# A four-layer kernel on one Trainium2 core: the start of the program in another order

## The reference

```python
x = x + mixer(layernorm(x), W_in, conv_w, ..., W_out)      # Mamba-2: 32 heads of 64, state 128
x = x + ffn(layernorm(x), w1, w2, w3)                      # ternary weights
x = x + attention(layernorm(x), W_qkv, W_o)                # 16 heads of 16, causal, ALiBi
x = x + moe(layernorm(x), gate_w, ..., shared_up_w, ...)   # 64 experts, 6 per token

# mixer
proj = einsum('bld,pd->blp', h, W_in)        # gate z 2048 | x 2048 | B 128 | C 128 | dt 32
hBC  = silu(conv4(proj[x, B, C]) + conv_b)   # depthwise, causal, 4 taps
dt   = softplus(dt + dt_bias);  dA = exp(-exp(A_log) * dt)
h_t  = dA_t * h_(t-1) + dt_t * x_t (outer) B_t;  y_t = C_t . h_t + D * x_t
out  = rmsnorm(y * silu(z)) @ W_out.T
# ffn
q(w) = clip(round(w / (mean(|w|) + 1e-8)), -1, 1)          # for w1, w2, w3: 256 x 704
```

## Time and profile before

| what | value |
|---|---|
| device time, median of 3 runs | 1346.67 us (1343.73 to 1346.82) |
| the profiled execution | 1346.53 us, span 1344.7 us |
| PE busy | 1132.3 us, 84% of the span |
| DVE busy | 911.7 us, 68% |
| ACT busy | 657.3 us, 49% |
| POOL busy | 566.6 us, 42% |
| chain that ended last | PE 47%, DVE 22%, ACT 9%, issue 9%, POOL 8%, DMA 4% |

### The profile page before, as it was taken

The page is one execution under the profiler, slowest core; times in us unless marked ns, Lnnn a source line. Parts: engine busy times, 40 slices in busy tenths (PEclk is TensorE's granted clock), DMA queues, the critical chain, the costliest instruction groups (busy, mean ns, idle before and its releaser), DMA issues.

```text
span 1344.7 us, 24377 instructions
## 1 busy us (share of the span) xinstructions
PE 1132.3 (84%) x8378; PEld 731.2 (54%) x8380; DVE 911.7 (68%) x1850; ACT 657.3 (49%) x1575; POOL 566.6 (42%) x725
## 2 busy tenths in 40 slices
PE   2799998898999888989899888989899879877940
PEld 2355556665555556665555566655555566653520
DVE  4488786565788885657887875657888765661417
ACT  3655434666555524757545335666555245611630
POOL 1255561220377761210677831201777712143750
PEclk9899999998999999999999998999999999978975
DMA  7365552300243314101343332002423534077988
GB/s 318 103 211 191 176 165 76 95 2 21 89 148 110 92 58 120 51 2 36 124 140 101 116 76 79 18 21 64 136 100 124 182 103 145 2 245 236 159 195 316
DMA packets 120137, 159.56 MB, mean 119 GB/s; under 512 B 11632, under 2 KB 82928, under 8 KB 119280
## 3 DMA queue, kind: packets, MB, share of 16 engines
q1 hardware_dynamic: 106384, 131.73, 31.3%
q0 software_dynamic: 9216, 19.98, 5.7%
q10 hardware_dynamic: 4416, 6.29, 1.3%
HBM read 104.55 MB, written 40.83 MB: 108 GB/s over the span
## 4 chain that ended last, share of the span: by engine, by line
PE 47%; DVE 22%; ACT 9%; issue 9%; POOL 8%; DMA 4%; SPq 0%; DVEq 0%; POOLq 0%; ACTq 0%
PE bank L1187 11%; DVE pool_c L1690 6%; PE bank L1229 5%; PE bank L1110 4%; PE bank L1410 3%; PE bank L1367 3%; PE bank L1395 3%; POOL xn L2207 2%; PE bank L1332 2%; POOL joint L2200 2%; DVE joint L1706 2%; DVE pool_c L1731 2%; PE bank L1216 2%; PE bank L1208 2%; PE bank L1223 2%
## 5 line engine op out<-in xcount | busy, mean ns | idle before, releaser
L1187 PE MATMUL bank<-xm,joint 128*128 128x512 f32 x544 | 271.0, 622 | 20.7 <-DVE pool_c L1690 15.6
L2200 POOL TENSOR_TENSOR joint<-joint 128x512 f32<-128x512 f32 x128 | 168.4, 1317 | 211.3 <-DVE joint L1706 208.0
L1690 DVE SCALAR_TENSOR_TENSOR pool_c<-bank,params,pool_c 128x511 f32<-128x511 f32 (+2 forms) x216 | 161.3, 747 | 73.8 <-ACT pool_c L812 68.2
L1187 PEld LDWEIGHTS bank<-xm,joint 128*128 128x128 f32 x544 | 99.2, 196 | 124.2 <-issue 93.1
L1891 DVE TENSOR_REDUCE nmax<-bank 128x1 f32<-128x384 f32 (+3 forms) x176 | 109.6, 637 | 60.6 <-PE bank L1368 59.8
L1229 PE MATMUL bank<-wout,pool_c 128*128 128x256 f32 x512 | 121.8, 381 | 3.4 <-DVE pool_c L1731 3.4
L851 ACT ACTIVATE joint<-bank,dt_ 128x64 f32<-128x64 f32 x512 | 111.6, 339 | 23.8 <-PE bank L1110 23.7
L1229 PEld LDWEIGHTS bank<-wout,pool_c 128*128 128x128 f32 x512 | 95.9, 190 | 36.6 <-issue 22.2
L821 ACT ACTIVATE pool_c<-pool_c 128x512 f32<-128x512 f32 x64 | 40.3, 629 | 141.8 <-DVE pool_c L1690 141.8
L2194 POOL DMA_INDIRECT xslot<-xrow,slots x96 | 97.2, 1012 | 26.6 <-issue 21.7
L1731 DVE TENSOR_TENSOR pool_c<-xn,pool_c 128x512 f32<-128x512 f32 x64 | 90.0, 1406 | 18.9 <-POOL xn L2207 18.9
(11 more groups left out here) (272 smaller groups left out, 2354.4 us busy)
## 6 DMA issues: line engine op xcount, KB each, us to landing
pool_b<-dA_rows SPq DMA_DIRECT2D x64, 256.0 KB, 3.3
pool_b<-dec_rows SPq DMA_DIRECT2D x96, 128.0 KB, 3.5
joint<-pool_b SPq DMA_DIRECT2D x96, 128.0 KB, 2.4
acc<-xrow SPq DMA_DIRECT2D x13, 640.0 KB, 6.3
joint<-dA_rows SPq DMA_DIRECT2D x32, 256.0 KB, 3.2
dA_late<-dA_rows SPq DMA_DIRECT2D x32, 256.0 KB, 4.0
joint<-acc SPq DMA_DIRECT2D x32, 256.0 KB, 6.8
xslot<-xrow SPq DMA_DIRECT2D x16, 321.0 KB, 4.7
```

The lines of the kernel that those rows point to most:

```text
L1187: last = mm(bank[:, :], win[:, k, col:col + P], xm[:, k, :], start=(k == 0), stop=(k == KD - 1))
L1690: ins = v.scalar_tensor_tensor(out=cv[:, n:L], in0=bank[:, 0:L - n], scalar=convw[:, ci, TAPS - 1 - n:TAPS - n], in1=cv[:, n:L], op0=ALU.m ...
L2200: M_ready.inc(p.tensor_tensor(M[u % 2][:, hs_, :], Lx[:, hs_, :], cbm[:, c * P:(c + 1) * P].unsqueeze(1).to_broadcast([P, 4, P]), ALU.mult))
```

## The change

The change touches only the start of the program, up to the first tiles of row 0.

1. SP issues the first part of `win` (x, B, C, dt) right after `params`, ahead of the FFN weights and masks. The z part keeps its place behind them.
2. PE waits only for that first part before `step_products`; the wait for the z part stands ahead of the first z tile.
3. `step_sums` moves behind the projection of tile `b`; on ACT `step_decays` moves behind tile `b`'s `tap`.
4. The quantisation moves into `between(None, 0)`. On ACT the three magnitude sums stand one behind `step_decays` and two behind `silu` of tile `c`. On PE their sum over partitions stands behind the projection of tile x1. On DVE masks, thresholds and the first weight stand behind the convolution of tile x1, the second and third weight behind that of tile x2. The six large DVE operations are now done weight by weight, each waiting for the one before.
5. `pro_dve` ends at 3. The last waits for it stand ahead of ACT's mixer steps, POOL's mixer steps and PE's FFN. `step_logs` waits only for 2, which the first DVE instructions give. SP no longer waits for `pro_act` ahead of the first decay loads.
6. The raw weights lie elsewhere, so that the first tiles do not write over them: the second in `pool_b`, the others and the masks in parts of `pool_a` that are written late; `low` is one buffer instead of three, in `pool_b`.

The arithmetic is the same. The diff, without the buffers' and thresholds' lines that only move:

```diff
@@ sync
             for name in ("consts", "params"):
                 w_small_loaded.inc(sp.dma_start(small[name][:, :], a[name]))
+            w_in_loaded[0].inc(sp.dma_start(win[:, :, INTER:PROJ], a["win"][:, :, INTER:PROJ]))
             for dst, src in ffn_loads:
                 w_ffn_loaded.inc(sp.dma_start(dst, src))
-            for lo, hi in ((INTER, PROJ), (0, INTER)):
-                w_in_loaded[lo == 0].inc(sp.dma_start(win[:, :, lo:hi], a["win"][:, :, lo:hi]))
+            w_in_loaded[1].inc(sp.dma_start(win[:, :, 0:INTER], a["win"][:, :, 0:INTER]))
...
-                else:
-                    sp.wait_ge(pro_act.sem, 2)
@@ scalar
+            def magnitude(i):
+                act.wait_ge(w_ffn_loaded.sem, 16 * len(ffn_loads))
+                act.wait_ge(pro_act.sem, 1 + i)
+                pro_act.inc(sa.activation(magnitudes, wf[i], ACT.Abs, accum_out=absum[:, i:i + 1]))
...
             def mixer_steps():
+                if b == 0:
+                    act.wait_ge(pro_dve.sem, PRO_DVE)
...
                 m(tap, tile_b)
+                if done is None:
+                    step_decays()
+                    magnitude(0)
                 m(read_rows)
...
                 m(silu, tile_c)
+                if done is None:
+                    magnitude(1)
+                    magnitude(2)
                 r(router_scores)
...
-            act.wait_ge(w_ffn_loaded.sem, 16 * len(ffn_loads))
-            for i in range(3):
-                last = sa.activation(pool_b[:, i * 1536:(i + 1) * 1536], wf[i], ACT.Abs, accum_out=absum[:, i:i + 1])
-            pro_act.inc(last)
-            act.wait_ge(pro_dve.sem, PRO_DVE)
+            act.wait_ge(pro_dve.sem, 2)
             step_logs()
-            step_decays()
@@ tensor
+            def weight_means():
+                pe.wait_ge(pro_act.sem, 4)
+                pro_pe.inc(mm(pb[5][:, 0:3], ones[:, :], absum, start=True, stop=True))
...
                 m(project_in, tile_b)
+                if done is None:
+                    step_sums()
...
                 m(project_in, ("x", 0, 1))
+                if done is None:
+                    weight_means()
                 m(unit_matrices)
...
+                if done is None:
+                    pe.wait_ge(w_in_loaded[1].sem, 16)
                 m(project_in, ("z", 0, 0))
...
-            for s in w_in_loaded:
-                pe.wait_ge(s.sem, 16)
+            pe.wait_ge(w_in_loaded[0].sem, 16)
             step_products()
-            step_sums()
@@ vector
+            def ternary(i):
+                link(v.tensor_scalar(low, wf[i], nthr[:, i:i + 1], None, ALU.is_lt))
+                last = v.scalar_tensor_tensor(out=wt[i], in0=wf[i], scalar=thr[:, i:i + 1], in1=low, op0=ALU.is_gt, op1=ALU.subtract)
...
                 r(best_groups)
+                if done is None:
+                    thresholds()
+                    ternary(0)
                 m(convolve, ("x", 0, 2))
+                if done is None:
+                    ternary(1)
+                    ternary(2)
@@ gpsimd
             def mixer_steps(done, coming):
+                if coming == 1:
+                    pool.wait_ge(pro_dve.sem, PRO_DVE)
```

More of the change, by code:

```diff
@@ L374, in build @@
         out_stored = signal("out_stored", 16)
-        PRO_DVE = 7
+        PRO_DVE = 3
         block = ctx.enter_context(nc.Block())
@@ L613, in build @@
                       for e in range(2)]
-        wf = [carve(pool_a, i * 1536, 1536) for i in range(3)]
+        wf = [carve(pool_a, 2048, 1536), carve(pool_b, 2048, 1536), carve(pool_a, 5120, 1536)]
         masks = carve(pool_a, 4608, 2 * P)
-        low = [carve(pool_a, 4864 + i * 768, 768, F16) for i in range(3)]
+        low = carve(pool_b, 6144, 768, F16)
+        magnitudes = carve(pool_a, 0, 1536)
         wt = [w.rearrange("p k n -> p (k n)") for w in (w1q[:, :, :], w2q[:, :, :], w3q[:, :, :])]
@@ L1281, in ffn @@
                 here = b
+                if b == 0:
+                    pe.wait_ge(pro_dve.sem, PRO_DVE)
                 norm_T(1, 0)
@@ L2035, in finish, with thresholds @@
                 add_shared()
+            def thresholds():
+                dve.wait_ge(w_ffn_loaded.sem, 16 * len(ffn_loads))
+                v.tensor_copy(maskb[:, :], masks[:, 0:P])
+                v.tensor_copy(maskTb[:, :], masks[:, P:2 * P])
+                dve.wait_ge(pro_pe.sem, 1)
+                link(v.tensor_scalar(thr, pb[5][:, 0:3], 1.0 / (FF * D), 1e-8, ALU.mult, ALU.add))
+                link(v.tensor_scalar(nthr, thr, -0.5, None, ALU.mult))
+                link(v.tensor_scalar(thr, thr, 0.5, None, ALU.mult))
+            def ternary(i):
+                link(v.tensor_scalar(low, wf[i], nthr[:, i:i + 1], None, ALU.is_lt))
+                last = v.scalar_tensor_tensor(out=wt[i], in0=wf[i], scalar=thr[:, i:i + 1], in1=low, op0=ALU.is_gt, op1=ALU.subtract)
+                if i < 2:
+                    link(last)
+                else:
+                    pro_dve.inc(last)
             def between(done, coming):
@@ L2080, in _ @@
             last = v.tensor_reduce(selcol[:, :], ident[:, 0:P:32], AX.X, ALU.add)
-            pro_dve.inc(last)
-            dve.wait_ge(w_ffn_loaded.sem, 16 * len(ffn_loads))
-            v.tensor_copy(maskb[:, :], masks[:, 0:P])
-            v.tensor_copy(maskTb[:, :], masks[:, P:2 * P])
-            dve.wait_ge(pro_pe.sem, 1)
-            pro_dve.inc(v.tensor_scalar(thr, pb[7][:, 0:3], 1.0 / (FF * D), 1e-8, ALU.mult, ALU.add))
-            dve.wait_ge(pro_dve.sem, 3)
-            pro_dve.inc(v.tensor_scalar(nthr, thr, -0.5, None, ALU.mult))
-            dve.wait_ge(pro_dve.sem, 4)
-            pro_dve.inc(v.tensor_scalar(thr, thr, 0.5, None, ALU.mult))
-            dve.wait_ge(pro_dve.sem, 5)
-            for i in range(3):
-                last = v.tensor_scalar(low[i], wf[i], nthr[:, i:i + 1], None, ALU.is_lt)
-            pro_dve.inc(last)
-            dve.wait_ge(pro_dve.sem, 6)
-            for i in range(3):
-                last = v.scalar_tensor_tensor(out=wt[i], in0=wf[i], scalar=thr[:, i:i + 1], in1=low[i], op0=ALU.is_gt, op1=ALU.subtract)
             pro_dve.inc(last)
```

2 lines of the change are left out of this document (removed).

## The result

The changed kernel takes 1336.11 us (median of 5 runs, 1332.61 to 1337.9), the kernel before in the same series 1344.8 (5 runs, 1343.73 to 1346.82). The ratio is 0.9927, with a 95% interval of 0.9906 to 0.9949: faster, by more than the 0.3% that can be told from no change. The forecast was 1336.9 and the range 1333.5 to 1341.5. The profiled run is the longest of its five, as the one before (1346.53) was near the longest of its.

A forecast was written before the change was run, and what follows sets the result against it. Early on, PE waits for `win`, queued behind the FFN weights, until 23.4 us. Gains of 10.7 and 1.5 less losses of 1.9 and 0.5 make 9.8, so 1346.67 becomes 1336.9 us; range 1333.5 to 1341.5.

The forecast's parts named there:

- The load order, 10.7: At the program's start: `win` lands at about 12.6 us, so step products start at 12.75 instead of 23.47, 10.7 earlier.
- Rival C: First part of `win` lands with the weights, at 18.4, 5.8 us later than forecast: 1342.7 us; chance 0.05.
- Tile b in the gap, 1.5: Tile `b` fills PE's idle gap before the step sums: 1.5 us more saved, 12.2 at the tap of `c`.
- I take the full rate: PE at tile `c`, behind the new wait: assumed 1.73 us rather than 3.41, an open bound of 1.7.
- rival B: The clock falls in PE's new gap, so tile `c` costs 1.7 us more: 1338.6 us; chance 0.25.
- The table load on the path: ACT's load for Exp, 1.28 us, no longer hidden behind tile `b`'s tap; PE waits from 21.0 to 22.8.
- Magnitudes two and three, 1.9: On ACT between the silu of `c` and x1's tap: 3.0 us against 1.1 of cover, 1.9 late.
- The sum over partitions, 0.5: On PE behind x1's projection, delaying the transposes of `b` and x0: 0.5 us lost, bounds 0 and 1.2.
- DVE's part, 0: Masks and weights fit DVE's idle times ahead of x2 and x3 (4.0 in 5.70, 5.6 in 7.73): cost 0.
- Rival D: The moved quantisation lies uncovered on the ACT, DVE, PE chain, and TensorE stays slow: 1352.5 us; chance 0.04.
- The queues, 0: Decay-row stores, `wout` scaling, z part of `win` and last `pro_dve` waits are all ready before needed: cost 0.
- Rival E: The start is earlier but the end is not, something with a fixed time taking the gain: 1346.7 us; chance 0.06.

The follow-up runs named there:

- experiment 1: Changed kernel with the FFN weights and masks loaded ahead of the first part of `win` again: median 1342.31 us, ratio to the kernel before 0.9981.
- experiment 4: Changed kernel with unread products (4, 6, 7, 8 and 7) in five of PE's waits: 1335.82 us in one run.
- experiment 8: Changed kernel with the second weight made ternary three times on DVE, 5.8 us more ahead of the convolution of x3: 1340.76 us in one run.
- experiment 11: The changed kernel itself, unaltered, timed again as control beside the combined kernel: median 1335.41 us, ratio to the kernel before 0.9936.
- Experiment 7: Changed kernel with the first weight made ternary twice on DVE, 2.9 us more ahead of the convolution of x2: 1336.03 us in one run.
- experiment 3: Changed kernel with the step sums and step decays ahead of tile `b` again: 1336.52 us in one run.
- experiment 2: Kernel before with only the load order changed, first part of `win` ahead of the FFN weights, z part last: median 1349.73 us, ratio 1.0039.
- experiment 10: The combined kernel: changed kernel with tile `c` ahead of the decay rows, x1's tap ahead of magnitudes two and three, weights' sum later, unread products: median 1329.38 us.
- 12: The combined kernel without its unread products, all else the same: median 1332.45 us, ratio to the kernel before 0.9913.
- experiments 5 and 6: Changed kernel with ACT's second magnitude moved ahead of tile `c`'s silu, identical program: 1331.74 us in a single run, then median 1334.48 of six.
- experiments 9: Changed kernel with tile `c` projected ahead of the decay rows on PE and tapped ahead of the first magnitude on ACT: 1334.37 us in one run.

## Why the prediction was right

**The load order, 10.7.** Right: 10.6. `xm` was done at 12.65, `win` landed at 12.7. Rival C (a landing at 18.4) is refuted by the row of 10.49 and by experiment 1, in which weights that stand ahead cost 6 us. Both orders landed as a queue that is served in order has them: 10.5 us after the issue with nothing of the weights ahead, 14.4 with all of them.

**Tile b in the gap, 1.5: the term that was mis-sized.** The step products ended at 16.4, the sums ran from 19.83 and the decay rows started at 22.93, all within 0.15 of the working. But the decay rows took 1.03 and not 0.69, tile `c` took 2.59 and not 1.73, and the tap came at 26.58, not 25.3: of the 10.95 saved there the load order has 10.6, so the term was 0.3. The step that failed is "I take the full rate", for which I had the 8 us of matmuls ahead of the wait.

In the profile of after those matmuls had not brought the full rate. Tile `b` (3.59), the sums (1.22; 0.71 in experiment 4) and the decay rows (1.03; 0.60 in experiment 8) all ran at the low level, and so did a part of tile `c`. The clock could not fall in the new wait, as rival B has it; it had not yet risen. B is what the second profile of the same program shows (experiment 11):

```profile
19.70 0.91 PE L1156 MATMUL bank<-a_,consts 128*128 128x128 f32 x4
22.80 0.60 PE L1117 MATMUL bank<-consts,pool_c 128*64 128x128 f32 x4 [2.19 <-POOL pool_c L2211]
23.24 5.29 PE L1198 MATMUL bank<-xm,joint 128*128 128x512 f32 x8
```

There the level rose within the sums (0.91) and the decay rows are at the full rate behind the wait, but then the granted clock is 0.50 from 24 to 26, and the tap came at 26.56. Experiment 7 has the same (0.50 from 24 to 26, tap 26.88). In experiment 8 the level rose in the wait and stayed, and the tap came at 25.30, as forecast. So over four profiles with the same list up to there the tap came at 25.30, 26.56, 26.58 and 26.88, against 26.68 in experiment 3, in which tile `b` isn't moved: the move was worth 1.4 in one and nothing in three. The prediction had left the rate of tile `c` open, and gave rival B a chance of 0.25 and 1.7 us. What decides which of the three ways a run takes, no experiment shows.

**The table load on the path.** 1.28 us at 20.85, with Exp 0.02 behind it, as the row of the silu had it. The extra 1.38 of the Trainium skill (ScalarE: Activation LUTs, "What ACT_TABLE_LOAD costs") isn't in the trace.

**Magnitudes two and three, 1.9.** Right: 10.95 saved at the tap of `c` and 9.01 at that of x1 make 1.94. From the start of the second to that of the third went 1.66 and not 1.48; each now waits for the one before.

**The sum over partitions, 0.5.** It was 0: between the tap of x1 (9.0) and the transposes behind it (9.0) nothing was lost. The transposes of tile `b` ran under the convolution of x1, my lower bound.

**DVE's part, 0.** Right: DVE is idle ahead of both convolutions in both profiles of the kernel after (3.38 and 1.92; 2.47 and 2.05). Experiments 7 and 8 show where the cover ends: the first goes 0.86 over it and the second 3.7, and the convolutions are late by that much. Rival D (1352.5) is refuted for this kernel. Its mechanism is real: experiment 2 is slower by 0.39% through it.

**The queues, 0.** The rows' stores were issued at 24.82, the first decay loads at 30.49, before 36.49 and 39.50; no engine waited for them.

**What was lost on the way.** Of 9.0 at the transposes 7.8 are left at the tap of x2: tile x2 fell into the low level (3.24 for four records, against 1.98 in the kernel before), the further 1.5 us that the range held. The low level at x3 came back too (5.40 for eight, before 6.57), so the saving stayed at 7.8. Experiment 4 puts the whole of these levels at 3 to 4 us of the scan's start, experiment 10 against 12 at 2.7, all by single profiles. The kept gain ahead of the scan is therefore 7.8 and not 9.8, 2 us less than I had.

**Why the time still fits.** The span is shorter by 8.6 and the medians by 8.7; the ratio's interval holds 6.9 to 12.6 us. My 9.8 was taken from a median of 1346.67 that three runs gave; five gave 1344.8. The forecast of 1336.9 is 0.8 high, with a gain 1.1 too large subtracted from a start 1.9 too high. That it lies so near is luck, since the two errors cancel; that it lies within the range is not, since the range had room for the low levels. Rival E (the gain swallowed later) is refuted: 7.93 of the gain were there at the first scan product and 8.6 at the end, and the 0.7 between is less than the stretch varies by.

## What to carry to other kernels

A load that is moved forward gains nothing while a later-landing load feeds work that stands in the same engine's list ahead of the first consumer; look for that work before the load is moved, and move both (apart: 0.2% faster and 0.4% slower, together 0.7% faster). Where a change fills or opens waits of TensorE of about 2 us, price the tiles behind them at both levels of the clock, and don't trust a single run for gains of that size. Cover on an engine is measured by doubling the work that lies in it; compare the end of the wait with the end of the extra work in the same profile, since the total can agree by luck (experiment 7).

## What the runs showed of the hardware

- The level of the clock isn't fixed by the program. One and the same program ran tile x2 in full rate (3.60 for eight) in one profile and partly at the low level (5.09) in another, behind the same idle time of 1.95 (experiments 5 and 6). The kernel after ran the step sums at the low level in one profile (1.22 us) and partly at the full one in the other (0.91).
- A DVE cast can be held by POOL. The cast of the masks takes 0.22 us by itself. In the combined kernel it began under POOL's scaling of `wout` and took 2.99, and ended 0.08 behind it; in the kernel without unread products it took 3.38 and in experiments 9, 5, 6 and 4 it took 1.27, 0.63, 0.36 and 0.34, each time to within 0.1 us behind the end of POOL's operation (here that of the combined kernel):

```profile
28.50 7.03 POOL L2322 TENSOR_TENSOR wout<-wout,params 128x4096 f32<-128x4096 f32 x1 [5.78 <-DMA wout<-in_wout]
```

  The convolution's rows ran under the same operation at their old 2.31 for three. The Trainium skill (SBUF — State Buffer, "SBUF: two separate sides") says that GpSimd and a VectorE operation in a two-port mode take a shared port pair as a lock for the whole instruction; the traces agree with the waiting; in which mode the cast runs, and that it is this port that it waits for, no run shows. In the kernel after the cast came 1.16 us behind the end of the scaling (28.57 + 7.03, cast at 36.76) and cost nothing. The prediction didn't see this: whoever moves the masks forward by more than 1.2 us runs into it.
